# A graph layer's one-hots: transposed by TensorE, or spread by a transfer and compared on VectorE

## The reference

```
ZU = einsum('nd,kdr->knr', Z, U)
zs, zd = ZU[:, src, :], ZU[:, dst, :]
logits = (zs * zd).sum(-1) / sqrt(R)
alpha = softmax of logits over the edges of each target node (segment max, exp, segment sum)
agg = segment_sum(alpha[..., None] * zs, dst)
ssa = einsum('k,knr,kdr->nd', softmax(head_w), agg, U)
Z_half = 0.5 * Z + 0.5 * ssa;  DZ = Z_half @ Dmat.T
grad = Z_half + 0.5 * (Z_half - DZ @ Dmat) @ Dmat
x = layernorm(x + relu(grad - 0.05))
```

## Time and profile before

| | us |
|---|---|
| median of 3 runs | 3708.65 |
| lowest, highest | 3697.53, 3719.24 |
| profiled execution, its own time | 3677.74 |
| its span | 3675.2 |
| TensorE matmul busy | 1971.2 (54%) |
| VectorE busy | 1919.5 (52%) |
| GpSimd busy | 1728.5 (47%) |
| ScalarE busy | 1168.6 (32%) |
| mean granted TensorE clock | 0.577 |

### The profile page before, as it was taken

The page is one execution under the profiler, slowest core; times in us unless marked ns, Lnnn a source line. Parts: engine busy times, 40 slices in busy tenths (PEclk is TensorE's granted clock), DMA queues, the critical chain, the costliest instruction groups (busy, mean ns, idle before and its releaser), DMA issues. The chain is left out here.

```text
span 3675.2 us, 61713 instructions
## 1 busy us (share of the span) xinstructions
PE 1971.2 (54%) x15251; PEld 1490.8 (41%) x15252; DVE 1919.5 (52%) x5864; ACT 1168.6 (32%) x3040; POOL 1728.5 (47%) x1832
## 2 busy tenths in 40 slices
PE   9345545454545445454545455464545454567776
PEld 9233333343434334343424243343433333444666
DVE  4444646454545546454545455464545454666477
ACT  1112323222232323322232233233232322334477
POOL 1544454445444444554544544445544444252662
PEclk7555555555555555555555555555555555577798
DMA  6212222121212212121212112121212121285343
GB/s 205 52 32 46 47 44 46 42 46 42 48 41 47 46 41 48 42 49 40 47 39 48 42 44 48 41 50 41 48 40 45 41 49 39 58 274 179 112 140 107
DMA packets 406593, 232.96 MB, mean 63 GB/s; under 512 B 284096, under 2 KB 371434, under 8 KB 406506
## 3 DMA queue, kind: packets, MB, share of 16 engines
q1 hardware_dynamic: 346666, 154.11, 15.4%
q0 software_dynamic: 59840, 77.87, 9.8%
HBM read 134.80 MB, written 42.55 MB: 48 GB/s over the span
## 5 line engine op out<-in xcount | busy, mean ns | idle before, releaser
L576 POOL DMA_INDIRECT arena<-z_table,sslot x1563 | 1492.0, 955 | 1646.2 <-SPq L418 1114.0
L1347 PE MATMUL bank<-arena 128*128 x4992 | 613.8, 222 | 637.7 <-issue 585.8
L1347 PEld LDWEIGHTS bank<-arena 128*128 128x128 bf16 x4992 | 457.5, 105 | 789.5 <-issue 697.0
L1584 ACT ACTIVATE arena<-bank 128x272 f32<-128x272 f32 x416 | 269.8, 661 | 1574.8 <-remote 970.4
L902 DVE TENSOR_TENSOR xin<-arena,bank 128x512 f32<-128x512 f32 x208 | 143.1, 688 | 1044.3 <-remote 588.2
L1561 ACT ACTIVATE acc<-xTb 128x68 f32 x1600 | 384.6, 312 | 306.6 <-issue 296.0
L1364 PE MATMUL bank<-xto,arena 128*128 128x68 bf16 x3328 | 321.6, 246 | 147.5 <-issue 147.4
L1335 PE MATMUL bank<-ident_b,arena 128*128 128x128 bf16 x1664 | 214.8, 310 | 339.4 <-remote 205.3
L1364 PE MATMUL bank<-arena 128*128 128x68 bf16 x1664 | 296.9, 243 | 120.2 <-issue 90.5
L1364 PEld LDWEIGHTS bank<-xto,arena 128*128 128x128 bf16 x3328 | 281.5, 132 | 166.9 <-issue 166.9
L1335 PEld LDWEIGHTS bank<-ident_b,arena 128*128 128x128 bf16 x1664 | 160.4, 141 | 399.6 <-remote 200.2
(11 more groups left out here) (264 smaller groups left out, 2543.6 us busy)
## 6 DMA issues: line engine op xcount, KB each, us to landing
arena<-arena SPq DMA_DIRECT2D x1660, 32.0 KB
arena<-z_table,sslot POOLq DMA_INDIRECT x1563
dspace<-in_xT SPq DMA_DIRECT2D x49, 256.0 KB
xmz_table<-agn SPq DMA_DIRECT2D x49, 256.0 KB
xmz_table<-arena SPq DMA_DIRECT2D x14, 896.0 KB
arena<-in_x SPq DMA_DIRECT2D x13, 896.0 KB, 11.4
out<-arena SPq DMA_DIRECT2D x12, 896.0 KB
xin<-in_xT SPq DMA_DIRECT2D x8, 896.0 KB
```

The costliest lines, as they stand in the source:

```text
L576: pool.indirect_dma_start(ring[:, e % RING, :], None, z_table, bass.IndirectOffsetOnAxis(ap=sslot[:, e:e + 1], axis=0)).then_inc(tiles_in[ ...
L1347: last = T.matmul(zd_ps[g % 2][:, u * KR:(u + 1) * KR], onehotT[:, g * G + u, :], z3[:, bass.ds(tiles[u], 1), s, :].rearrange("p a c -> p ...
L1584: A.activation(sums[:, :, 1 + q * Q:1 + (q + 1) * Q].rearrange("p c j -> p j c"), sum_ps[q % 2][:, 0:Q * AW].rearrange("p (j c) -> p j c", ...
```

## The change

The transposed one-hots no longer come from TensorE. A table `place_rows` holds each edge's local node number in bf16, one row of 128 a step; it is written once at the start. For each block SyncE loads its 32 rows into all 128 partitions of `onehotT` (8 KB to a partition, 1 MB in all), and VectorE compares them in place with the partition number, four instructions of 128x1024, ahead of the one-hots of the next block. The transposes on TensorE and the copies on ScalarE go. The load of block b waits for all expansions of the block before it (`zd_ready`), since there is one buffer.

`zd_ps` now has four banks, one a group; the x product uses the fourth. Expansions 0 to 2 of block b+1 stand in the places of the transposes, between the small matmuls of the chain. Expansion 3 stands after sums 0 to 3.

SyncE loads the eight counts of a block at once (`load_needs`), and its order in `turn` is: groups 0 and 1, x step, resets, groups 2 and 3, store of the x product, tiles of x, places.

The diff, cut to its core:

```diff
@@ layout, banks
+        place = oflat[:, 2 * S:2 * S + S // 2].bitcast(BF16).rearrange("p (g e) -> p g e", e=P)
-        tr_ps = [p[:, :].bitcast(BF16) for p in psum[2:4]]
-        zd_ps = psum[4:6]
+        zd_ps = psum[2:6]
@@ sync
+            def load_places(b):
+
+                if not (type(b) is int and b == 0):
+                    sp.wait_ge(zd_ready, NG * b)
+                    sp.nop(nofuse=True)
+                sp.dma_start(onehotT.rearrange("p j e -> p (j e)"),
+                             spread(place_rows[bass.ds(b * B, B), :].rearrange("(a j) e -> a (j e)", a=1), 0, P)).then_inc(places_in, 16)
+
+            def load_needs(b):
+
+                _, need = nc.values_load_multi_w_load_instructions(
+                    needs[0:1, bass.ds(b * NG * 2, 2 * NG)], engines=[mybir.EngineType.SP], min_val=16 * G, max_val=16 * G * EG)
+                return need
@@ copy_steps
-                    need = [sp.value_load(needs[0:1, bass.ds((b * NG + g) * 2 + i, 1)], min_val=16 * G, max_val=16 * G * EG) for i in range(2)]
                     for i in range(2):
-                        sp.wait_ge(tiles_in[i], need[i])
+                        sp.wait_ge(tiles_in[i], need[2 * g + i])
@@ sync, start
+            sp.wait_ge(place_ready, 1)
+            sp.dma_start(place_rows.rearrange("(g p) e -> p g e", p=P), place[:, :, :]).then_inc(places_out, 16)
@@ turn
+                need = load_needs(b)
                 for g in range(2):
-                    copy_steps(b, h, g, uses)
+                    copy_steps(b, h, g, uses, need)
                 sp.wait_ge(x_ready, b - 1)
+                sp.nop(nofuse=True)
                 load_resets(b, h)
+                for g in range(2, NG):
+                    copy_steps(b, h, g, uses, need)
                 if store:
...
                 if load:
                     load_tiles(b - 1, 1 - h)
-                for g in range(2, NG):
-                    copy_steps(b, h, g, uses)
+                if places:
+                    load_places(b + 1)
@@ sync, blocks 0 and 1
+            sp.wait_ge(places_out, 16)
+            sp.wait_ge(tab_read, 5)
+            load_places(0)
             sp.wait_ge(prep_read, 6)
             load_tiles(0, 0)
+            load_places(1)
+            need = load_needs(1)
             for g in range(NG):
-                copy_steps(1, 1, g, 1)
+                copy_steps(1, 1, g, 1, need)
+            load_places(2)
@@ vector
+            def make_onehotT(b, h):
+
+                dve.wait_ge(places_in, 16 * (b + 1))
+                V.tensor_scalar(first_col[:, h:h + 1], onehotT[:, 0, 0:1], pno[:, 0:1], None, ALU.is_equal).then_inc(v_step, 1)
+                dve.wait_ge(v_step, vn.next())
+                for g in range(NG):
+                    part = onehotT[:, g * G:(g + 1) * G, :].rearrange("p j e -> p (j e)")
+                    V.tensor_scalar(part, part, pno[:, 0:1], None, ALU.is_equal).then_inc(oneT_ready, 1)
@@ vector, period, after L970
                 if more:
+                    make_onehotT(b + 1, 1 - h)
                     copy_indices(b + 1, 1 - h)
                 next_onehot(0)
@@ tensor, expand
-                    pe.wait_ge(zd_used, NG * b + g - 1)
+                    pe.wait_ge(zd_used, NG * (b - 1) + g + 1)
@@ tensor, period
-                next_transposes(0)
+                if more:
+                    expand(b + 1, 0)
                 pe.wait_ge(carry_ready, b + 1)
...
-                next_transposes(1)
+                if more:
+                    expand(b + 1, 1)
                 pe.wait_ge(heads_ready, b + 1)
...
-                next_transposes(2)
+                if more:
+                    expand(b + 1, 2)
                 pe.wait_ge(back_ready, b + 1)
...
-                next_transposes(3)
...
-                if more:
-                    expand(b + 1, 0)
-                    if dense:
-
-                        pe.wait_ge(xmz_copied, b)
-                    expand(b + 1, 1)
                 add_up(b, h, 0, 4)
                 if more:
-                    expand(b + 1, 2)
-                add_up(b, h, 4, 6)
-                if more:
+                    if dense:
+
+                        pe.wait_ge(xmz_copied, b)
                     expand(b + 1, 3)
-                add_up(b, h, 6, 8)
+                add_up(b, h, 4, 8)
@@ scalar, period
-                if more:
-                    copy_onehots(b + 1, 1 - h, 0)
...
-                    A.activation(xmz, zd_ps[1][:, :], ACT.Copy, bias=-ETA * LAM).then_inc(xmz_copied, 1)
+                    A.activation(xmz, zd_ps[NG - 1][:, :], ACT.Copy, bias=-ETA * LAM).then_inc(xmz_copied, 1)
```

More of the change, by code:

```diff
@@ L767, in _ @@
             dve.wait_ge(v_step, vn.next())
+            dve.wait_ge(tab_ps, 1)
+            V.tensor_copy(place[:, :, :], dloc[:, :, :]).then_inc(place_ready, 1)
             V.memset(lastcol[:, 0:1], 0.0)
@@ L1326, in _ @@
             pe.wait_ge(prep_read, 6)
-            def transpose_onehots(b, h, g):
-                if g >= 2 or not (type(b) is int and b == 0):
-                    pe.wait_ge(oneT_ready, NG * b + g - 1)
-                pe.wait_ge(onehot_ready, NG * b + g + 1)
-                for u in range(G):
-                    last = T.transpose(tr_ps[g % 2][:, u * P:(u + 1) * P], onehot[:, h, g * G + u, :], ident_b[:, :])
-                last.then_inc(oneT_ps, 1)
             def expand(b, g):
                 tiles = steps_of(b, g)
-                if g >= 2 or not (type(b) is int and b == 0):
-                    pe.wait_ge(zd_used, NG * b + g - 1)
+                if not (type(b) is int and b == 0):
+                    pe.wait_ge(zd_used, NG * (b - 1) + g + 1)
                 pe.wait_ge(oneT_ready, NG * b + g + 1)
@@ L1346, in expand @@
                     for s in range(ZP):
-                        last = T.matmul(zd_ps[g % 2][:, u * KR:(u + 1) * KR], onehotT[:, g * G + u, :],
+                        last = T.matmul(zd_ps[g][:, u * KR:(u + 1) * KR], onehotT[:, g * G + u, :],
                                         z3[:, bass.ds(tiles[u], 1), s, :].rearrange("p a c -> p (a c)"), start=(s == 0), stop=(s == ZP - 1))
@@ L1368, in period @@
             def period(b, h, xe_uses=None, more=True, dense=True):
-                def next_transposes(g):
-                    if more:
-                        transpose_onehots(b + 1, 1 - h, g)
                 def multiply_x(t):
                     for c in range(DC):
-                        last = T.matmul(zd_ps[1][:, t * D:(t + 1) * D], xe[:, 1 - h, c, t * P:(t + 1) * P], mz[:, c, :],
+                        last = T.matmul(zd_ps[NG - 1][:, t * D:(t + 1) * D], xe[:, 1 - h, c, t * P:(t + 1) * P], mz[:, c, :],
                                         start=(c == 0), stop=(c == DC - 1))
@@ L1411, in period @@
                     multiply_x(1)
+                add_up(b, h, 0, 4)
                 if more:
-                    expand(b + 1, 0)
                     if dense:
                         pe.wait_ge(xmz_copied, b)
-                    expand(b + 1, 1)
-                add_up(b, h, 0, 4)
-                if more:
-                    expand(b + 1, 2)
-                add_up(b, h, 4, 6)
-                if more:
                     expand(b + 1, 3)
-                add_up(b, h, 6, 8)
-            for g in range(NG):
-                transpose_onehots(0, 0, g)
+                add_up(b, h, 4, 8)
             pe.wait_ge(z_rest, 4)
@@ L1608, in period @@
                 A.activation(ratio[0:1, 1, :], ratio[0:1, 0, :], ACT.Exp, scale=float(R) ** -0.5).then_inc(ratio_ready, 1)
-                if more:
-                    copy_onehots(b + 1, 1 - h, 3)
                 if dense:
@@ L1624, in _ @@
             act.wait_ge(tab_read, 8)
-            for g in range(NG):
-                copy_onehots(0, 0, g)
             period(0, 0, dense=False)
```

36 lines of the change are left out of this document (13 added, 23 removed).

## The result

The changed kernel takes 3888.18 us (median of 3, 3875.6 to 3906.24) against 3708.65: a ratio of 1.049, 95% interval 1.0407 to 1.0572. It is slower. Its profiled span is 3886.4, that of before 3675.2: 211 more.

The account below looks back on a forecast made before the run. A ring of SyncE's slots, GpSimd's gathers and VectorE's chain bounds it. Every second block caught adds 5.8 us a block, 290 over 50, plus 10 at the start, on 3677.7; with 31 offset, 4010, range 3470 to 4500.

Parts of the forecast that it names:

- What bounds the kernel: Block loop: a ring of SyncE freeing slots, GpSimd gathering (37.6 us) and waiting (20.8), VectorE's chain; 58.4 a block.
- starved stretches: Times when gathers nearly stop other engines, from some 5.5 us after a run's start to 3.3 after its end.
- The first run's wait: GpSimd's wait for SyncE before a block's first run of gathers: 17.5 us against 9.56 in the kernel before.
- The second run's wait: GpSimd's wait after two joined runs catch VectorE's chain: 3.3 + 8.8 + 6.8 = 18.9 us.
- Which blocks are caught: Gathers stall VectorE's chain in about every second block, 74.0 against 55.1 us, mean 64.6; chance 0.34.
- the start: Beginning of the kernel: 10 us added for block 1's copies waiting on block 0's expansions and writing a table.
- The chain's own length: VectorE, fourth product to x step without starvation: 12.9 + 3.0 compares + 3.6 transfer + 4 expansions = 23.5 us.
- The order of copies: SyncE copies groups 2 and 3 earlier, removing GpSimd's third wait (7.74 us) and joining runs to 20 us or more.
- Caught in every block: Rival: gathers stall VectorE's chain in all blocks, 15.2 x 50 + 10 + 31, so 4480 us; chance 0.20.
- Not caught: Rival: VectorE's chain ends before the gathers stall it, -3.7 x 50 + 10, giving 3533 us; chance 0.30.
- the mean kept: Rival: GpSimd's next wait gives back whatever VectorE's chain gains or loses, 3690 to 3727 us; chance 0.08.
- Gathers held up by VectorE: Rival: new 1024-column VectorE operations delay GpSimd for their whole length, 2.8 us a block, 140, so 3850; chance 0.08.

## Why the prediction was right or wrong

Direction and range held: 3888 against 4010, in 3470 to 4500. By its own steps:

**What bounds the kernel** held: the gathers are as long as ever, and the difference of the spans is that of GpSimd's waits. The pauses show that the starved stretches are the cost, not a sign of it.

**The first run's wait**, forecast 17.5, is 18.3. Its parts stood in the right order: end of the stretch, sums and fourth expansion (1461.06 and 3.19), the transfer's issue, eight copies.

**The second run's wait**, forecast 18.9 when the chain is caught, is 8.3 to 8.5: this is the step that failed. I had the third group's copies start 1.5 after the x step. They don't wait for it. I had described the wait in `turn` as one for the x step of the block before; it is `x_ready` at `b - 1`, reached with the x step of block `b - 2`, long past when SyncE comes to it. What had tied the copies to the last x step was the store of the x product, which the new order put behind them. They start at 1496.43, as the stretch ends, while the chain does its last steps. From 1484.1 on SyncE takes one small step after another, 0.7 to 1.6 us apart, and none is a long wait: it is starved itself. One of its small register instructions for these copies, in the stretch and behind it:

```profile
L440 SPq FUSED_REGOPS  x1: 698/698/698, 1491.4 to 1491.4; - x1
```

```profile
L440 SPq FUSED_REGOPS  x1: 52/52/52, 1502.0 to 1502.0; - x1
```

The wait is that of a caught block only where the old order is put back: 19.0. Also, the chain is caught at the heads' scan, with 2.9 left to the x step (1498.14 to 1501.08), not 8.8.

**Which blocks are caught**: I took every second one, of 74 and 55. Nearly all are caught (39 heads' scans wait), but a caught block is 66. That the total came so near is luck, two errors that nearly cancel: mean 63.2 against my 64.6, 4.4 more than before against 5.8. Of the 122 that I was too high, 66 are this term; 25 are the start, where the first x step came 15 earlier instead of 10 later; 31 is the offset between median and profiled run, which the changed kernel doesn't have (3888 and 3886).

**The chain's own length**, forecast 23.5 from fourth product to x step, can be read in one block of the changed kernel that no stretch caught. VectorE:

```profile
1528.69 0.69 DVE L940 TENSOR_TENSOR xin<-arena,bank 128x512 f32<-128x512 f32 x1 [8.45 <-PE bank L1378]
...
1532.08 0.42 DVE L1008 TENSOR_TENSOR_SCAN xin<-xTb,bank 128x128 f32<-128x128 f32 x1 [1.79 <-PE bank L1411]
...
1533.80 0.21 DVE L928 TENSOR_SCALAR first_col<-arena,pno 128x1 f32<-128x1 bf16 x1 [1.29 <-DMA arena<-place_rows]
...
1543.95 0.56 DVE L1036 TENSOR_TENSOR_SCAN back<-rnext,bank 1x32 f32<-1x32 f32 x4 [1.09 <-PE bank L1424]
...
1547.86 0.16 DVE L1047 COPY dcol<-bank 128x1 f32<-128x1 f32 x1 [1.60 <-issue]
...
1548.64 0.29 DVE L1051 TENSOR_TENSOR xin<-bank,xin 128x128 f32<-128x128 f32 x1
```

It is 19.95, against 12.9 before. The compares took 1.9 with the small one, not 3.0. The transfer left 1.3 open, not 3.6. The waits that the expansions in the gaps cause here are 1.09 and 1.60, not 4. All three terms were sized too high, each inside its bounds. I had no term for the 1.79 before L1008 (0.37 in the earlier trace rows): TensorE does sums until then, ahead of the transpose of the logits. With the expansions out of the gaps the time is the same; the compares weren't taken out. Of the transfer, what cost was not VectorE's wait of 1.3 but SyncE's for the fourth expansion, ahead of its issue: that wait stood in the prediction, inside the first run's 17.5.

For the four compares the Trainium skill (VectorE: DVE Perf Modes, the perf-mode tier table) had given 1.9 as an estimate; VectorE's row L932 above has 1.68 for them, so the rule was the better price, and the eight small compares a poor one.

**The order of copies** I called the reason why runs join. It isn't, alone: no more of them joined. What joins them in the changed kernel I can't say. Undoing the order, the expansions or the transfer leaves 88, 88 and 83% in long runs. Left are the single load of counts and the sums that now follow each other closer; neither was tried alone.

**The rivals.** Caught in every block was right on the blocks and wrong by 8 us on their length. Not caught, and the mean kept, fell. Gathers held up by VectorE fell too: 952 ns against 955. In the changed kernel no four compares stand beside a gather of the loop, so that says little; in the version with pauses and the early expansion they sometimes do. GpSimd's timeline there:

```profile
1251.52 1.27 POOL L604 DMA_INDIRECT arena<-z_table,sslot  x1 [0.30 <-issue]
1253.10 0.94 POOL L604 DMA_INDIRECT arena<-z_table,sslot  x1 [0.30 <-issue]
```

and VectorE's:

```profile
1251.40 1.67 DVE L938 TENSOR_SCALAR arena<-arena,pno 128x1024 bf16<-128x1024 bf16 x4
```

The gather beside the four compares took 1.27 instead of 0.94. The Trainium skill's lock (SBUF — State Buffer, SBUF: two separate sides) may be seen here, but it is worth 0.3 us, less than one of the four compares (0.42), and not the 1.67 for which VectorE was at them. Over all 62 gathers of that version that overlap a compare the mean is 1.08, against 0.97 for the others.

## What to carry to other kernels

Where a run of indirect gathers slows every other engine, the length of the runs is a thing to tune: 3.5 us in which GpSimd gathers nothing after every eight gave 6.5% in one kernel and 11% in the other, though it added work to an engine on the ring. Ask of each step beside such a run whether it can be issued before the stretch begins; one expansion, moved into an idle spot of TensorE ahead of it, gave back all that the change had lost, because another queue stood at a wait for it. And before pricing a wait by its place in the code, check which count it waits for: a wait for last block's event orders nothing.

## What the runs showed of the hardware that was not expected

That the stretches stop about 2 us after GpSimd goes from gathers to iotas, and that TensorE then does 55 matmuls in 5.4 us; so it is the gathers, not a busy GpSimd. That SyncE is starved as well: a register instruction of 0.05 us took 0.70. That VectorE can stand idle until the end of a stretch although the matmuls it needs have run: 5.18 us in the block above. Whether the signal is late or VectorE's own next instruction, the rows don't tell.

What inside the chip is short during a run stays open. DMA share is 0.17 in the worst stretch, 0.48 in another. Row copies beside the gathers, which I took for the mark of the hard kind, are not needed for it. In the kernel with the pause of 14 iotas SyncE's timeline has its row copies up to here:

```profile
1114.85 15.92 SPq L451 DMA_DIRECT2D arena<-arena  x16
```

The next are issued at 1143.78. In between lies the stretch above from 1133.5 to 1141.0, with no matmul, ScalarE idle from 1129.3 to 1140.96 and a small instruction of SyncE at 1137.92 that took 0.71; other transfers ran then (DMA share 0.48). The row copies were never taken away or moved to another queue. The profile's instruction queue moved 14 packets, 0.11 MB, between 500 and 3000 us of the kernel before, so no row shows code loading that fills these stretches; whether all of it goes through that queue isn't shown.
